# Softmax loop of an early-fusion kernel: distances ahead of weights, scores ahead of remainders, first evacuation earlier, output extremes in pieces

## The reference, cut to what matters

```python
attn = einsum('bhnd,bhmd->bhnm', q, k) * hd ** -0.5
attn, s_attn = fq_act(attn)                  # rounded to 255 levels over the whole tensor
x_int = x / scale - max(x / scale);  x_int = maximum(x_int, 30 * x0_int)
q = floor(x_int / x0_int);  r = x_int - x0_int * q         # quotient and remainder
z = r * (r + b_int) + c_int;  exp_int = floor(z * exp2(30 - q))
sm = round(exp_int.sum(-1) / exp_int)        # then rounded to a power of two, 2 ** -qlog
o = einsum('bhnm,bhmd->bhnd', attn, v)
o, _ = fq_act(o)                             # needs the smallest and largest element of all o
```

## Time and profile before

| What | Value |
|---|---|
| median of 3 runs | 1095.77 us (1094.6 to 1095.95) |
| the profiled execution | 1094.12 us |
| its span, first to last instruction | 1092.3 us |
| busy over the span: PE, DVE, ACT, POOL | 767.7, 803.8, 523.8, 365.3 us |
| granted TensorE clock, 442 to 642 us | 0.50 to 0.55 of full speed |
| granted TensorE clock, from 788 us on | 0.94 to 1.00 |
| DVE busy in 500 to 560 us | 52.5 of 60 us |
| PE, ACT, POOL busy there | 49.1, 46.8, 15.9 of 60 us |

### The profile page before, as it was taken

How to read it: one execution, slowest core, us unless ns; L and a number is a source line. 1 busy time by engine, 2 the same in 40 slices (tenths; PEclk the granted TensorE clock), 3 DMA queues, 4 the chain that set the end, 5 groups by cost and what they waited for, 6 DMA issues and landing times.

```text
span 1092.3 us, 24142 instructions
## 1 busy us (share of the span) xinstructions
PE 767.7 (70%) x7852; PEld 594.8 (54%) x7852; DVE 803.8 (74%) x1834; ACT 523.8 (48%) x1069; POOL 365.3 (33%) x370
## 2 busy tenths in 40 slices
PE   3699894266725772377888862306299999999998
PEld 2698894155613441144545541206177777777777
DVE  3334551689977999688888879997577777777776
ACT  3122340134427432377777773438155555555554
POOL 2120000358812110122222221000066666666665
PEclk9999898567665555555555555555599999999999
DMA  7942622200002220112222217000000100000000
GB/s 191 263 134 58 190 84 62 86 14 0 0 0 74 73 73 15 46 30 39 44 38 38 44 18 240 9 0 2 16 10 24 32 15 30 23 22 23 22 28 17
DMA packets 114142, 58.11 MB, mean 53 GB/s; under 512 B 75656, under 2 KB 107568, under 8 KB 113968
## 3 DMA queue, kind: packets, MB, share of 16 engines
q1 hardware_dynamic: 112768, 51.24, 18.5%
q0 software_dynamic: 1328, 6.30, 2.0%
HBM read 29.61 MB, written 9.83 MB: 36 GB/s over the span
## 4 chain that ended last, share of the span: by engine, by line
PE 49%; DVE 17%; issue 11%; ACT 9%; SPq 6%; DMA 4%; POOL 2%; DVEq 0%; ACTq 0%; POOLq 0%
PE ps L1392 42%; ACT R L631 5%; PE ps L1552 4%; DMA R<-h_rows 2%; ACT ps L744 2%; DVE M L1090 2%; DVE M L1091 2%; SPq L473 2%; PE ps L1466 1%; ACT R L634 1%; DVE R L1184 1%; DVE R L1288 1%; DVE R L1080 1%; SPq L433 1%; DMA h_rows<-R 1%
## 5 line engine op out<-in xcount | busy, mean ns | idle before, releaser
L1392 PE MATMUL ps<-R 128*128 128x192 f16 (+8 forms) x3618 | 460.9, 281 | 32.3 <-DVE R L896 13.2
L1392 PEld LDWEIGHTS ps<-R 128*128 128x128 f16 (+4 forms) x3618 | 349.2, 114 | 119.2 <-issue 55.9
L623 POOL TENSOR_TENSOR R<-R 128x256 f32<-128x256 f32 x238 | 195.7, 829 | 188.7 <-DVE R L1369 187.1
L1369 DVE TENSOR_TENSOR R<-R,ps 64x256 f32<-64x256 f32 (+1 forms) x272 | 114.0, 419 | 62.9 <-ACT R L839 43.6
L839 ACT ACTIVATE R<-ps 128x256 f32<-128x256 f32 x238 | 91.1, 383 | 136.5 <-PE ps L1392 129.4
L1392 PE MATMUL ps<-M 32*128 32x68 bf16 (+2 forms) x1152 | 99.1, 245 | 74.5 <-DMA M<-R 54.6
L631 ACT ACTIVATE R<-ps 68x896 bf16<-68x896 bf16 (+7 forms) x140 | 94.6, 678 | 111.9 <-PE ps L1466 45.4
L631 ACT ACTIVATE R<-R 128x256 f16<-128x256 f32 (+5 forms) x281 | 125.5, 448 | 21.5 <-POOL R L569 19.1
L1392 PEld LDWEIGHTS ps<-M 32*128 32x128 bf16 (+2 forms) x1152 | 63.4, 116 | 124.1 <-issue 72.3
L634 ACT ACTIVATE R<-R,sc 64x512 f16<-64x512 f32 (+12 forms) x106 | 82.8, 838 | 94.0 <-POOL R L586 41.1
L1376 DVE TENSOR_TENSOR R<-R 128x256 f16<-128x256 f32 x238 | 112.8, 475 | 20.1 <-ACT R L631 18.0
(11 more groups left out here) (235 smaller groups left out, 980.6 us busy)
## 6 DMA issues: line engine op xcount, KB each, us to landing
R<-in_x_dram SPq DMA_DIRECT2D x12, 576.0 KB, 7.5
M<-R SPq DMA_DIRECT2D x16, 260.0 KB, 2.4
M<-R SPq DMA_DIRECT2D x32, 130.0 KB, 2.0
R<-h_rows SPq DMA_DIRECT2D x4, 816.0 KB
R<-h_rows SPq DMA_DIRECT2D x1, 3264.0 KB, 14.1
R<-R SPq DMA_DIRECT2D x17, 192.0 KB, 2.5
out_dram<-R SPq DMA_DIRECT2D x17, 192.0 KB, 2.0
R<-w_split SPq DMA_DIRECT2D x1, 3072.0 KB, 20.7
```

What stands on the lines that cost most here:

```text
L623: pool.tensor_tensor(hs[0:rows, m % HB, :], hr[0:rows, m % HB, :], other, ALU.mult).then_inc(sem("squared"), 1)
L1369: last = tt(hc[rows, m % HB, :], hr[rows, m % HB, :], ps[rows, 2 + e % 2, 0:256], ALU.mult)
L1392: return pe.matmul(o, a, b, start=start, stop=stop, skip_group_check=True)
```

## The change: what it does

1. ScalarE's list: `evac_first` goes from behind `log_sums` to behind `ratios`; `evac_second` and `evac_o` change places, so that the output is evacuated last.
2. VectorE's list: `distances`, last before, goes ahead of `weights`.
3. TensorE's list: `second_scores` goes ahead of `remainders`.
4. The eight reductions for the output's extremes become twelve, cut at groups 14, 26 or 28. Three of them are issued inside VectorE's pipeline, in the drain steps 32 and 33; the nine others follow it. The memset of their tile goes ahead of the pipeline.

No lag, wait or buffer of the moved functions is changed.

```diff
+        OPARTS = [(0, 14, 0, True), (0, 14, 0, False), (14, 26, 0, True), (14, 26, 0, False),
+                  (0, 14, 1, True), (0, 14, 1, False), (14, 28, 1, True), (14, 28, 1, False),
+                  (26, 32, 0, True), (26, 32, 0, False), (28, 32, 1, True), (28, 32, 1, False)]
...
-            pipeline(act, [(ratios, 3), (log_weights, 2), (squares, 1), (log_sums, 2), (evac_first, 4), (evac_o, 6), (evac_second, 4)], 32)
+            pipeline(act, [(ratios, 3), (evac_first, 4), (log_weights, 2), (squares, 1), (log_sums, 2), (evac_second, 4), (evac_o, 6)], 32)
...
+            omx = extr.rearrange("p m k g -> p (m k g)")
+
+            def output_extreme(first, last, m, largest):
+                k = OPARTS.index((first, last, m, largest)) // 2
+                r, part = C1 if m else P, oT[m][:, first * 2 * N:last * 2 * N]
+                dve.wait_ge(sem("o_out"), last)
+                to = omx[0:r, k + (0 if largest else 6):k + (1 if largest else 7)]
+                dve.tensor_reduce(to, part, X, ALU.max if largest else ALU.min, negate=not largest).then_inc(sem("o_extreme"), 1)
+
+            def early_extremes(g, par, half):
+                if isinstance(g, int) and g == 30:
+                    output_extreme(*OPARTS[0])
+                if isinstance(g, int) and g == 31:
+                    output_extreme(*OPARTS[1])
+                    output_extreme(*OPARTS[2])
+
+            ch(dve.memset(extr, 0.0))
             pipeline(dve, [(clamp, 1), (quotients, 1), (powers, 1), (rounded, 3), (prob_bits, 3),
-                           (weight_sums, 2), (weights, 1), (distances, 0)], 32)
-
-            early = 28 * 2 * N
-            omx = extr.rearrange("p m k g -> p (m k g)")
-            ch(dve.memset(extr, 0.0))
-            for k, groups, t in ((0, 28, slice(0, early)), (1, 32, slice(early, T))):
-                dve.wait_ge(sem("o_out"), groups)
-                for m, o in enumerate(oT):
-                    r = C1 if m else P
-                    dve.tensor_reduce(omx[0:r, 2 * k + m:2 * k + m + 1], o[:, t], X, ALU.max)
-                    last = dve.tensor_reduce(omx[0:r, 4 + 2 * k + m:5 + 2 * k + m], o[:, t], X, ALU.min, negate=True)
-            ch(last)
-            ch(dve.tensor_reduce(sc[:, O_MX:O_MX + 2], omx[:, 0:8].rearrange("p (m k) -> p m k", m=2), X, ALU.max))
+                           (weight_sums, 2), (distances, 0), (weights, 1), (early_extremes, 2)], 32)
+
+            for part in OPARTS[3:]:
+                output_extreme(*part)
+            dve.wait_ge(sem("o_extreme"), len(OPARTS))
+            ch(dve.tensor_reduce(sc[:, O_MX:O_MX + 2], omx[:, 0:12].rearrange("p (m k) -> p m k", m=2), X, ALU.max))
...
-            pipeline(pe, [(turn_first, 4), (remainders, 1), (second_scores, 0), (turn_second, 4), (sum_v, 5)], 32)
+            pipeline(pe, [(turn_first, 4), (second_scores, 0), (remainders, 1), (turn_second, 4), (sum_v, 5)], 32)
```

## The result

The changed kernel took 1103.17 us (median of seven, 1099.64 to 1112.32) against 1095.95 (1094.6 to 1097.73) for the kernel before beside it: ratio 1.0077, interval 1.0044 to 1.011. It is slower. A second set gave 1.0087 (1.0055 to 1.0119). The forecast was 1079.5, range 1071 to 1090.

What follows compares the result with a forecast made beforehand. The prediction took a ScalarE–TensorE ring of 6.3 us as the bound, with SP's issue next (step 5.95). Gains of 8.0 + 2.4 + 5.1 = 15.5 us led from 1094.12 to 1078.6, or 1080.3 from the median; named 1079.5, range 1071 to 1090.

Steps and rivals of the forecast that it cites:

- What bounds the kernel now: Softmax loop: a ring of waits round ScalarE and TensorE, 6.3 us, sets the step of 6.245; VectorE only waits.
- The ScalarE edit: Softmax loop: first evacuation earlier, output last; ring with TensorE falls to 5.77 us, ring with GpSimd is 5.58.
- A: Rival, 14%: SP's issue shortens and does not hold the loop; step 5.77 us, execution 1073 to 1074.5.
- B: Rival, 20%: GpSimd and VectorE stretch each other on every loop step; step 6.1 to 6.4 us, execution 1083 to 1090.
- D: Slower rival, 7%: the load's landing decides the loop; at 3.6 us landing the step is 6.62, execution 1098.
- C: Rival, 12%: a missed ring keeps the loop's old step; only start and drain pay, 7.5 us, execution 1087 to 1088.
- The TensorE edit: Loop: scores go ahead of remainders and wait for the load; SP's issue, 5.91 us, plus 0.04 for jolts, sets 5.95.
- The VectorE edit: Loop: distances fill the wait before weights; VectorE's own step is 5.50 us, 0.75 to give back if nothing else slows.
- GpSimd beside VectorE: Loop: clamp would meet GpSimd's subtraction and wait for its end; ring 5.71 us, or 4.80 without the wait.
- The start: First four loop steps, not all parts present: 22.4 us against 24.8, a gain of 2.4.
- The drain: After the loop: VectorE ends 5.9 us earlier, but SP's last load holds the barrier, so the gain is 5.1.
- The sum: Whole execution: 8.0 steady loop, 2.4 start and 5.1 drain give 15.5 us off, to 1079.5.

Runs made afterwards that it cites:

- e9: The kernel before with only distances put ahead of weights on VectorE: step 6.272 us (6.255 before), total 1092.6 us.
- e4: The changed kernel with the output's evacuation still last but at lag 5 instead of 6: step 5.944 us, median 1077.18 us, ratio 0.9801.
- e5: e4 with three spreads of v instead of four, so its output is not the reference's: step 5.633 us, total 1069.3 us.
- e6: e4 with GpSimd's subtraction on 4 of 13 slots, so some probabilities are wrong: step 5.953 us, total 1073.9 us.
- e7: e4 with distances behind weights again on VectorE: step 6.287 us, total 1095.6 us.
- e3: The changed kernel with the output's evacuation ahead of the second evacuation: step 6.350 us, median 1085.66 us, ratio 0.9895.
- e12: e4, complete, with one of four spreads of v issued by ScalarE instead of SP: step 5.687 us, median 1074.72 us, ratio 0.9821.
- e8: The kernel before with only the twelve reduction pieces, three in the drain: step 6.247 us, total 1100.3 us.
- e11: e4, complete, with one of four spreads of v issued by GpSimd instead of SP: step 6.169 us, median 1091.73 us, ratio 0.9965.
- e1: The kernel before with only ScalarE's new order: step 6.55 us, total 1097.5 us.

## Why the prediction was wrong, point by point

- **What bounds the kernel now: right.** The ring of ScalarE and TensorE held the step; e9 shows that VectorE's wait was its effect and not a reserve.
- **The ScalarE edit: this step failed.** The prediction said "the output last" and counted the new ring as 1.09, 0.81, 0.13, 0.95, 1.10, 1.66, 0.03 = 5.77. The 0.13 between second evacuation and turn was the broken term. TensorE's order has `sum_v` between them, and `sum_v` waits for the output. In the trace after, from the end of the evacuation (534.93) to the turn (536.38) it is 1.45: output until 535.26, handover 0.14, `sum_v` 0.81, 0.16. Put in, 5.77 becomes 7.09; 7.04 was measured. On the other parity the same stretch is 1.22 (528.14 to 529.36), which gives 6.86; 6.79 was measured. The forecast had the wait of `sum_v` for the output at nothing, without a reason. In the trace of before that wait had 0.51 to spare and stood in no row. Rivals A, B and D kept the same omission. C allowed for a ring that had been missed, but one that keeps the old step, not one that lengthens it by 0.67. D, the slower one, named a DMA's landing, which never came into play (waits of 0.4 at the longest in e4).
- **The TensorE edit: the bound was right once the output was out of the way.** SP's issue, 5.91 plus 0.04, set the step: 5.944 in e4, confirmed by e5 and e6. That the 0.04 fits is luck. It was added for jolts among rings of near length, but SP's own parts make it up in e4: 3.64 from the spreads to the next load, 1.49 to its third DMA, and 0.81 instead of 0.78 to the spreads. The ring of ScalarE and TensorE without the output was 0.14 too long: the handover is 0.05 and the turn 0.89 to the next start (e5), 5.63. That of ScalarE and GpSimd was 0.05 too short: 5.63 too. In e5 squares wait for nothing and ratios wait for the subtraction in every step (17.9 us, 23 times); which of the two equal rings holds e5's step is not shown.
- **The VectorE edit: right that it pays only if nothing else turns slower.** e7 puts it at 0.34 a step in company, e9 at nothing alone.
- **GpSimd beside VectorE: right that clamp is held, too high in size.** Clamp lasts 1.12 in most steps, and the subtraction stays at 1661 to 1664 ns, never stretched. In the changed kernel, e3, e4, e5 and e12 clamp starts between 0.78 and 1.42 into the subtraction and each time ends 0.24 to 0.26 after it. A clamp that began only at the subtraction's end would end 0.45 after it, as the forecast had it; so by an estimate 0.2 of it is already done. e6 shows that it costs e4's step nothing. The Trainium skill's rule (SBUF — State Buffer, "SBUF: two separate sides"), that the one that starts first holds the other for a whole instruction, fits this end, which does not depend on the start; the trace of before could not show it. Rival B, both stretched, is refuted.
- **The start: right but for size.** The first four steps took 21.9 us (4.80, 6.08, 5.47, 5.52), forecast 22.4, before 24.8. The outputs begin in step 6; from the seventh interval on the weights come every 6.8 to 7.1 us, but for the last one.
- **The drain: nearly right.** 3.9 came back instead of 5.1, in the changed kernel and in e8 alike. VectorE is done 6.0 earlier after the last weights, where 5.9 was forecast. That `sum_v` and so SP's last loads would come 1.1 earlier did not hold in the changed kernel: SP's last issue ends 24.9 after the last weights, before 24.5. `sum_v` waited for the output there too. In e4, without this wait, SP ends at 23.1 and the gain is 5.7.
- **The sum.** 12.0 lost against 10.4 forecast as won in the loop. Of the difference of 22.4, the one wait makes 205.6 - 181.5 = 24.1 us (after against e4), more than all. The prediction's sum has two slips that do not bear on this: rival A's upper end is 1074.7 by its own terms, and rival B's step 5.71 + 2 x 0.37 = 6.45, not 6.4 or 6.36, which would put its end at 1092 to 1094.

## What to carry to other kernels

When an instruction moves back in its engine's order, list every semaphore that it signals and find each waiter in the code, also those that no row of the trace shows: a wait that was met early is invisible until its cover is gone. Where a buffer is single, an evacuation put last in the step can close a ring with the next writer. One lag less took the whole wait away, a new place in the order only part of it (e4 against e3). When one engine's idle time ends at another's result, work put into it may only move the wait (e9), unless the ring that brings the result is shortened too.

## What the runs showed of the hardware that was not expected

- A DMA of the same shape issued by GpSimd took 1.25 us to issue and landed 4.2 us after; issued by ScalarE it took 0.70, by SP 0.73 (medians). A VectorE instruction of 0.51 us that began inside GpSimd's issue lasted 1.00 to 1.28 and ended 0.17 to 0.20 after the issue (e11).
- A VectorE instruction of 0.45 us that began inside a GpSimd instruction of 1.66 us ended 0.25 us after it, whether it had begun 0.78 or 1.42 into it.
- The reload of rows from memory in an unchanged stage lasted 23 to 30 us, and the issue ahead of it 10.6 to 14.9; the start of the loop moved by up to 12.9 us between executions, some 10 of it by these two (e1 against e8). Against this, 31 steps of the loop repeated to the tenth of a microsecond (205.6 twice). A change of under 1% is read from the stage, not from one total.
